# A GRU scan of 256 steps: the input product of r, z and n as one matmul of 192 columns, two pairs of steps ahead, over three sets of PSUM banks

## The chip, the cores and the metric

The kernel runs on one core of one Trainium2 chip. The metric is the time of one execution on the device in microseconds (us), median over several runs. TensorE (PE in the profile, PEld for its weight loads), VectorE (DVE), ScalarE (ACT), GpSimd (POOL) and SyncE (SP, which issues DMAs) each work through an instruction stream of their own, in order, and meet by semaphores.

## What is computed

`x` is 16 batches of 256 steps of 512 channels. First each channel is convolved over time with its own 16 taps (causally; the taps of a channel are its 16 batch values of `cond`) and the result is added to `x`. Then a GRU runs over the 256 steps, with `cond` as the first state, and its states are added to that `x`:

```python
gi = x @ W_ih + b_ih          # 512 -> 3 * 512, known ahead of the step
gh = h @ W_hh + b_hh          # needs the state of the step before
r = sigmoid(i_r + h_r)
z = sigmoid(i_z + h_z)
n = tanh(i_n + r * h_n)
h = (1 - z) * n + z * h
```

All of it is float32.

## The kernel before

**Layout.** The 512 channels are four chunks c of 128, and a chunk is four column groups j of 32 on the PE. State and `x` are stored with channels on partitions. The output channels are worked in two halves f (256 channels each), so that one half's gates can be computed while the PE is on the other.

**PE, one step t** (L321 to L340). `recur(t, f, c)` (L286) multiplies the state, as the 32 stationary columns (16 batches of two steps, one of which is zero), with 192 columns of `whh`: r, z and n of half f. It is issued for eight pairs (f, c) in a fixed order, of which the first needs `s_h[0]` (half 0 of the state before) and the fourth `s_h[1]`. Behind them come four of the eight calls of `product(m + 1, t % 2, c)` (L262): the input product of the next pair of steps, half 0 in the even step and half 1 in the odd one. A product is two sets of four matmuls: 128 columns for r and z into `pg[m % 2][f]`, at L278, and 64 columns for n into a bank of its own, `pin[m % 2]`, at L281. The sums of r and z are made in PSUM on top of the product. The part of n of the input has to stay apart from that of the state, as the state's is multiplied by r first. `turn` (L295) makes, for steps 16 to 79 of x, the convolution on the PE in four sets of 16 rounds, which are spread over the steps named in `ROUNDS`.

**ACT** first seeds the PSUM banks with the biases (`seed`, L344: two copies of 192 columns at L353 and one of 128 at L354 for each pair, at the end of the odd steps), since the matmuls only add. Per step and half it computes sigmoid for r and z (L379), 1 - z (L381) and tanh (L384).

**DVE** has in each step, in this order (L503 to L519): for half 0 the transposes of r and z (`transpose_rz`, L446) and of the state's n (`transpose_n`, L450) out of PSUM and the scan that gives r * h_n + i_n (`scan_n`, L458); the transposes of half 1; `scan_h` of half 0 (L471), which gives the new state and releases the PE by `s_h[0]`; `scan_n` and `scan_h` of half 1, which gives `s_h[1]`. Then, in odd steps, `transpose_in` (L441): the input's n of the next pair, 128 columns out of `pin`. Last come parts of the convolution for later steps: `spread` (L437), and `long` (L423), one instruction per step or so from step 13 to 206 (`SPANS`).

**POOL** multiplies z by the state (L253) and adds the state to x for the output (L247). **SP** loads weights and x and stores the output in its own order.

The only place at which the PE waits for DVE in a step is for the state:

```python
pe.wait_ge(s_h[0], t + 1)
recur(t, 0, 0)
recur(t, 0, 1)
recur(t, 1, 0)
pe.wait_ge(s_h[1], t + 1)
```

Of the kernel before, what the change touches and what calls it, by code (L numbers as in the profile page):

```python
# [32 lines left out]
M2 = T // 2  # L33
HN, END = 2 * CH * D, 3 * CH * D
STORES = [(n * TB, (n + 1) * TB) for n in range(NB - 1)] + [(T - 16, T - 8), (T - 8, T - 2), (T - 2, T)]


def build(nc, x, cond, w_ih, w_hh, b_ih, b_hh, out):
    assert J * D == P
    ctx = ExitStack()  # L40
    with ctx:  # L41
# [23 lines left out]
        bhh = sb("bhh", [P, 3 * C])  # L65
        bcol = sb("bcol", [P, H, 3, CH])
        bc = sb("bc", [P, H, END])
        bcn = sb("bcn", [P, C * D])
# [4 lines left out]
        gn = sb("gn", [P, 2, H, CH, B, 2])  # L73
        rz = sb("rz", [P, H, 2, HB, 2])
# [32 lines left out]
        s_x1 = sem("s_x1")  # L107
        s_seed = sem("s_seed")
        s_gi = sem("s_gi")
        s_tin = sem("s_tin")  # L110
        s_gh = halves("s_gh")
# [45 lines left out]
        def _(sp):  # L157
# [103 lines left out]
        def _(pe):  # L261
            def product(m, f, c):  # L262

                if f == c == 0:
                    pe.wait_ge(s_seed, 3 * (m + 1))
                    if 2 * m < FEW:
                        pe.wait_ge(s_first, len(FIRST))
                    elif 2 * m < TB:
                        pe.wait_ge(s_first, len(FIRST) + len(REST))
                        pe.wait_ge(s_pa, K)  # L270
                    elif 2 * m < LONG[0][0]:
                        pe.wait_ge(s_x1, 2 * NT * ((2 * m - TB) // W2 + 1))
                    else:
                        pe.wait_ge(s_long, len(EVERY) * sum(a <= 2 * m for a, _ in LONG))
                w = wih[:, c, :, :].rearrange("p (g k) (j d) -> p j g k d", g=3, j=J)[:, :, :, f * CH:(f + 1) * CH]
                xx = x1_of(c, 2 * m, 2 * m + 2)
                for j in range(J):
                    pe.matmul(pg[m % 2][f][D * j:D * (j + 1), 0:HN], xx, w[:, j, 0:2],  # L278
                              start=False, stop=True, skip_group_check=True)
                for j in range(J):  # L280
                    i = pe.matmul(pin[m % 2][D * j:D * (j + 1), f * CH * D:(f + 1) * CH * D], xx, w[:, j, 2],  # L281
                                  start=False, stop=True, skip_group_check=True)
                if f == H - 1 and c == C - 1:
                    i.then_inc(s_gi, 1)

            def recur(t, f, c):  # L286

                for j in range(J):
                    i = pe.matmul(pg[t // 2 % 2][f][D * j:D * (j + 1), 0:END],  # L289
                                  hp[:, t % 2, 2 * c + 1 - t % 2:2 * c + 3 - t % 2, :, 1].rearrange("p u b -> p (u b)"),  # L290
                                  whh[:, c, :].rearrange("p (g j f n) -> p j f g n", g=3, j=J, f=H)[:, j, f],
                                  start=False, stop=True, skip_group_check=True)
                return i
# [16 lines left out]
            pe.wait_ge(s_clear, 1)  # L310
            for q in range(2):
                for bank in (pg[q][0], pg[q][1], pin[q]):
                    pe.matmul(bank[:, :], zeros[:, 0:P], zeros[:, :], start=True, stop=True).then_inc(s_bits, 1)
            for _ in range(WARM):
                pe.matmul(pcv[:, 0:512], zeros[:, 0:P], zeros[:, :], start=True, stop=True)
            for f in range(H):
                for c in range(C):
                    if f == 0:
                        pe.wait_ge(s_wih[c], 16)
                    product(0, f, c)  # L320
            for t in range(T):  # L321
                m = t // 2
                for c in range(C if t == 0 else 0):
                    pe.wait_ge(s_whh[c], 16)
                pe.wait_ge(s_h[0], t + 1)
# [17 lines left out]
        def _(act):  # L343
            def seed(m):  # L344

                if m < 2:
                    act.wait_ge(s_bits, 6)
                    act.wait_ge(s_bc, H + 1)
# [3 lines left out]
                for f in range(H):  # L352
# [18 lines left out]
            act.activation(pre[:, :], cnd[:, 0, :], ACT.Sigmoid)  # L371
            seed(0)
            seed(1)
            act.wait_ge(s_zero, 4)
            for t in range(T):
                u = slice(t % 2 * B, (t % 2 + 1) * B)
                for f in range(H):
# [6 lines left out]
                    act.activation(nzh[:, f, ::2, :, 0], chunks(an[:, f, :, 1]), ACT.Tanh).then_inc(s_n[f], 1)  # L384
                if t % 2 and t + 3 < T:
                    seed((t + 3) // 2)

        @block.vector
        def _(dve):
# [48 lines left out]

            def transpose_in(m):
                dve.wait_ge(s_gi, m + 1)  # L440
                dve.transpose(gn[:, :, :, :, :, 1].rearrange("p u f c b -> p (f c) u b"),  # L441
                              pin[m % 2][:, 0:C * D]).then_inc(s_tin, 1)

            def transpose_rz(t, f):
                dve.wait_ge(s_gh[f], t + 1)
                dve.transpose(gt[:, f, :, :].rearrange("p c r -> p (c r)"),  # L446
                              pg[t // 2 % 2][f][:, 0:HN]).then_inc(s_trz[f], 1)

            def transpose_n(t, f):
                dve.transpose(gn[:, :, f, :, :, 0].rearrange("p u c b -> p c u b"),  # L450
                              pg[t // 2 % 2][f][:, HN:END]).then_inc(s_tn[f], 1)

            def scan_n(t, f):

                dve.wait_ge(s_rz[f], t + 1)
                dve.wait_ge(s_tn[f], t + 1)
                dve.wait_ge(s_tin, t // 2 + 1)
                dve.tensor_tensor_scan(an[:, f].rearrange("p n s -> p (n s)"),  # L458
                                       rz[:, f, 0].rearrange("p n s -> p (n s)"),
                                       gn[:, t % 2, f].rearrange("p c b s -> p (c b s)"),  # L460
                                       0.0, ALU.mult, ALU.add).then_inc(s_an[f], 1)
# [21 lines left out]
            dve.wait_ge(s_small, 32)  # L483
            dve.tensor_copy(bcol[:, :, 2, :], bhh[:, 2 * C:].rearrange("p (f k) -> p f k", f=H)).then_inc(s_bcol, 1)
            for g in range(2):
                dve.tensor_tensor(bcol[:, :, g, :], bih[:, g * C:(g + 1) * C].rearrange("p (f k) -> p f k", f=H),
                                  bhh[:, g * C:(g + 1) * C].rearrange("p (f k) -> p f k", f=H),
                                  ALU.add).then_inc(s_bcol, 1)
            dve.wait_ge(s_bcol, 3)
            for f in range(H):  # L490
                dve.transpose(bc[:, f, :].rearrange("p (k d) -> p k d", d=D),
                              bcol[:, f].rearrange("p s k -> p (s k)").unsqueeze(2).to_broadcast([P, 3 * CH, D])
                              ).then_inc(s_bc, 1)
            dve.transpose(bcn[:, :].rearrange("p (k d) -> p k d", d=D),
                          bih[:, 2 * C:].unsqueeze(2).to_broadcast([P, C, D])).then_inc(s_bc, 1)
            dve.wait_ge(s_xs, 16)
# [4 lines left out]
            dve.wait_ge(s_zero, 4)  # L501
            transpose_in(0)
            for t in range(T):  # L503
# [48 lines left out]
```

## Time and profile before

| | before |
|---|---|
| median of 3 runs | 1063.55 us (1062.34 to 1065.3) |
| profiled execution, own time | 1064.67 us |
| its span | 1062.9 us |
| PE busy | 1035.6 us, 97% |
| DVE busy | 781.8 us, 74% |
| ACT busy | 410.1 us, 39% |
| POOL busy | 246.5 us, 23% |
| mean granted clock of the PE | 0.996 |

The span is the part of the execution that the profile shows; 1.77 us of the execution's own time lie around it. A matmul of the program appears as two records in the profile, each with its weight load (16384 records for 8192 `recur` matmuls). Matmul ends are modelled, so the length of the PE's work is best read from one start to another.

### The profile page before, as it was taken

What the parts mean: (1) busy time and instruction counts of PE and PEld (TensorE: products, weight loads), DVE (VectorE), ACT (ScalarE), POOL (GpSimd) and SP (SyncE); (2) the same over time, 40 slices, a digit from 0 to 9 for tenths busy, and PEclk for the clock granted to TensorE, in tenths of its full rate; (3) what the DMA queues carried; (4) which work ended last, traced back from release to release, by engine and by line L of the source; (5) the groups of instructions that cost most, each with busy time, mean ns of one, the idle gap of its engine ahead of it and who ended that gap; (6) DMA issues with size and microseconds to landing.
All of it is one profiled execution on the core that took longest, in us unless ns stands there. A gap on an engine that the chain in (4) does not pass through costs nothing.

```text
span 1062.9 us, 74575 instructions
## 1 busy us (share of the span) xinstructions
PE 1035.6 (97%) x33336; PEld 964.1 (91%) x33336; DVE 781.8 (74%) x2474; ACT 410.1 (39%) x1939; POOL 246.5 (23%) x796
## 2 busy tenths in 40 slices
PE   8979998999999999999999999999999999999997
PEld 4867897999999988999999999999999999999997
DVE  8535786788888878888888877777777765555554
ACT  4323333334334334334444344343443434334443
POOL 6211221222222222222222222222222222222222
PEclk9999999999999999999999999999999999999999
DMA  7886003000000030000000000000000000000000
GB/s 273 80 154 63 24 5 113 13 5 24 5 25 5 11 95 5 24 5 25 5 4 25 5 25 5 24 5 5 25 4 24 5 17 12 4 24 5 25 15 13
DMA packets 96225, 32.60 MB, mean 31 GB/s; under 512 B 84512, under 2 KB 93344, under 8 KB 95904
## 3 DMA queue, kind: packets, MB, share of 16 engines
q1 hardware_dynamic: 95472, 27.73, 11.6%
q8 instruction: 261, 4.28, 1.7%
q14 instruction: 60, 0.49, 0.2%
q10 hardware_dynamic: 432, 0.11, 0.0%
HBM read 19.35 MB, written 8.49 MB: 26 GB/s over the span
## 4 chain that ended last, share of the span: by engine, by line
PE 96%; issue 2%; DMA 2%; SPq 0%; DVE 0%; POOLq 0%; ACT 0%; DVEq 0%
PE pg L289 64%; PE pg L278 21%; PE pin L281 10%; DMA whh<-w_hh 2%; PE pcv L304 1%; SPq L184 0%; SPq L186 0%; DVE hp L471 0%; SPq L182 0%; DVE gn L450 0%; SPq L181 0%; POOLq L41 0%; DVE an L458 0%; ACT nzh L384 0%; DVEq L469 0%
## 5 line engine op out<-in xcount | busy, mean ns | idle before, releaser
L289 PE MATMUL pg<-whh,hp 128*32 128x192 f32 x16384 | 752.9, 327 | 18.9 <-issue 14.9
L289 PEld LDWEIGHTS pg<-whh,hp 128*32 128x32 f32 x16384 | 609.6, 110 | 76.7 <-issue 25.2
L278 PE MATMUL pg<-wih,x 128*32 128x128 f32 x8192 | 391.6, 273 | 0.8 <-issue 0.7
L281 PE MATMUL pin<-wih,x 128*32 128x64 f32 x8192 | 363.4, 219 | 0.0
L253 POOL TENSOR_TENSOR nzh<-rz,hp 128x32 f32<-128x32 f32 x512 | 158.2, 309 | 806.5 <-ACT rz L379 806.5
L281 PEld LDWEIGHTS pin<-wih,x 128*32 128x32 f32 x8192 | 344.4, 110 | 0.0
L379 ACT ACTIVATE rz<-gt 128x64 f32<-128x64 f32 x512 | 136.4, 266 | 514.2 <-DVE gt L446 486.7
L278 PEld LDWEIGHTS pg<-wih,x 128*32 128x32 f32 x8192 | 326.6, 110 | 5.4 <-issue 1.5
L446 DVE STREAM_TRANSPOSE gt<-pg 128x128 f32<-128x128 f32 x512 | 162.0, 316 | 143.9 <-PE pg L289 135.1
L471 DVE TENSOR_TENSOR_SCAN hp<-zcp,nzh 128x96 f32<-128x96 f32 x512 | 173.2, 338 | 78.2 <-ACT nzh L384 78.0
L458 DVE TENSOR_TENSOR_SCAN an<-rz,gn 128x64 f32<-128x64 f32 x512 | 149.3, 292 | 52.7 <-ACT rz L379 51.8
L384 ACT ACTIVATE nzh<-an 128x32 f32<-128x32 f32 x512 | 121.5, 237 | 127.9 <-DVE an L458 127.9
L423 DVE SCALAR_TENSOR_TENSOR x<-xb,cnd,x 128x1024 f32<-128x1024 f32 (+1 forms) x120 | 134.1, 1118 | 0.0
L381 ACT ACTIVATE zcp<-gt 128x32 f32<-128x32 f32 x512 | 111.2, 217 | 0.0
L450 DVE STREAM_TRANSPOSE gn<-pg 128x64 f32<-128x64 f32 x512 | 107.2, 209 | 0.0
L247 POOL TENSOR_TENSOR x<-x,hp 128x64 f32<-128x64 f32 x256 | 81.8, 319 | 0.9 <-DVE hp L471 0.7
L423 DVE SCALAR_TENSOR_TENSOR x<-tz,cnd,x 128x1024 f32<-128x1024 f32 x60 | 75.2, 1253 | 0.0
L353 ACT ACTIVATE pg<-bc 128x192 f32<-128x192 f32 x256 | 72.9, 317 | 0.0
L441 DVE STREAM_TRANSPOSE gn<-pin 128x128 f32<-128x128 f32 x128 | 37.5, 293 | 0.0
L354 ACT ACTIVATE pin<-bcn 128x128 f32<-128x128 f32 x128 | 33.4, 261 | 0.0
L304 PE MATMUL pcv<-tz,xw 128*32 128x64 f32 x512 | 11.2, 220 | 1.7 <-issue 1.7
L407 DVE SCALAR_TENSOR_TENSOR x<-xs,cnd,x 128x192 f32<-128x192 f32 (+11 forms) x45 | 12.8, 361 | 0.0
(38 smaller groups left out, 87.6 us busy)
## 6 DMA issues: line engine op xcount, KB each, us to landing
out<-x SPq DMA_DIRECT2D x15, 512.0 KB, 4.8
xw<-x SPq DMA_DIRECT2D x32, 128.0 KB, 4.9
wih<-w_ih SPq DMA_DIRECT2D x4, 768.0 KB, 8.2
whh<-w_hh SPq DMA_DIRECT2D x4, 768.0 KB, 13.5
xb<-x SPq DMA_DIRECT2D x1, 2528.0 KB, 11.7
tz<-x SPq DMA_DIRECT2D x1, 2528.0 KB, 12.4
xb<-x SPq DMA_DIRECT2D x1, 2016.0 KB, 11.0
tz<-taps SPq DMA_DIRECT2D x8, 128.0 KB, 5.0
```

The source lines that it names most:

```text
L253: pool.tensor_tensor(nzh[:, f, ::2, :, 1], chunks(rz[:, f, 1, :, 1]), h_of(t - 1, slice(f * CH, (f + 1) * CH)), ALU.mult).then_inc(s_zh[f], 1)
L278: pe.matmul(pg[m % 2][f][D * j:D * (j + 1), 0:HN], xx, w[:, j, 0:2], start=False, stop=True, skip_group_check=True)
L281: i = pe.matmul(pin[m % 2][D * j:D * (j + 1), f * CH * D:(f + 1) * CH * D], xx, w[:, j, 2], start=False, stop=True, skip_group_check=True)
L289: i = pe.matmul(pg[t // 2 % 2][f][D * j:D * (j + 1), 0:END], hp[:, t % 2, 2 * c + 1 - t % 2:2 * c + 3 - t % 2, :, 1].rearrange("p u b -> p ...
L379: act.activation(rz[:, f, :, :, 1].rearrange("p g (c b) -> p (g c) b", b=B), gt[:, f, :, u], ACT.Sigmoid).then_inc(s_rz[f], 1)
L381: act.activation(zcp[:, f, ::2, :, 1], gt[:, f, CH:, u], ACT.Sigmoid, scale=-1.0).then_inc(s_zc[f], 1)
L384: act.activation(nzh[:, f, ::2, :, 0], chunks(an[:, f, :, 1]), ACT.Tanh).then_inc(s_n[f], 1)
L423: dve.scalar_tensor_tensor(o, xx[:, c, (K - 1 - lag) * B:(K - 1 - lag + n) * B], cnd[:, c, K - 1 - lag:K - lag], o if lag else now, ALU.mu ...
L446: dve.transpose(gt[:, f, :, :].rearrange("p c r -> p (c r)"), pg[t // 2 % 2][f][:, 0:HN]).then_inc(s_trz[f], 1)
L450: dve.transpose(gn[:, :, f, :, :, 0].rearrange("p u c b -> p c u b"), pg[t // 2 % 2][f][:, HN:END]).then_inc(s_tn[f], 1)
L458: dve.tensor_tensor_scan(an[:, f].rearrange("p n s -> p (n s)"), rz[:, f, 0].rearrange("p n s -> p (n s)"), gn[:, t % 2, f].rearrange("p c ...
L471: dve.tensor_tensor_scan(hp[:, (t + 1) % 2, a:a + n].rearrange("p c b s -> p (c b s)"), zcp[:, f, 0:n].rearrange("p c b s -> p (c b s)"), ...
```

## The change

The input product of a pair is one matmul of 192 columns per (f, c, j), for r, z and n together, into the one bank `pg[m % 3][f]`. A bank now holds, in 256 columns, the state's n (0 to 64), r and z (64 to 192) and the input's n (192 to 256). `recur` writes columns 0 to 192, `product` columns 64 to 256. `pin` is gone, and there are three sets of two banks instead of two sets of three (with `pcv` seven banks in both). Before the first step the products of pairs 0 and 1 are made, and step t makes half `t % 2` of pair `m + 2`.

`seed` is two copies of 256 columns for each pair, three pairs ahead. `transpose_in` is one instruction of 64 columns for each half: half 0 of the next pair at the end of the even step, half 1 at the end of the odd step, behind `scan_h(t, 1)`. `gn`, its target, has two buffers. Since `transpose_in` reads a bank that `recur` of the next pair writes, the PE waits in even steps for both transposes before the first `recur`. `whh` is loaded with n's columns first, in two DMAs per chunk. The rounds of `turn`, the `spread`s and the spans of `long` are one or two steps earlier.

```diff
-HN, END = 2 * CH * D, 3 * CH * D
+RZ, IN, END = CH * D, 3 * CH * D, 4 * CH * D
+Q = 3
...
-        pg = [[pb(f"pg{q}{f}") for f in range(H)] for q in range(2)]
-        pin = [pb(f"pin{q}") for q in range(2)]
+        pg = [[pb(f"pg{q}{f}") for f in range(H)] for q in range(Q)]
...
-        ROUNDS = {(0, 0): (7, 9), (0, 1): (11, 12), (1, 0): (16, 20), (1, 1): (28, 32)}
-        TURNED = {(0, 0): (9, 11), (0, 1): (12, 14), (1, 0): (20, 28), (1, 1): (32, 40)}
-        SPANS = [(13, 78), (78, 142), (142, 206)]
+        ROUNDS = {(0, 0): (7, 8), (0, 1): (10, 11), (1, 0): (16, 20), (1, 1): (28, 32)}
+        TURNED = {(0, 0): (8, 10), (0, 1): (11, 12), (1, 0): (20, 28), (1, 1): (32, 40)}
+        SPANS = [(12, 76), (76, 140), (140, 204)]
...
-                sp.dma_start(whh[:, c, :], w_hh[:, c, :]).then_inc(s_whh[c], 16)
+                sp.dma_start(whh[:, c, 0:F], w_hh[:, c, 2 * F:]).then_inc(s_whh[c], 16)
+                sp.dma_start(whh[:, c, F:], w_hh[:, c, 0:2 * F]).then_inc(s_whh[c], 16)
...
-                if f == c == 0:
-                    pe.wait_ge(s_seed, 3 * (m + 1))
+                if c == 0:
+                    pe.wait_ge(s_seed[f], m + 1)
...
                 for j in range(J):
-                    pe.matmul(pg[m % 2][f][D * j:D * (j + 1), 0:HN], xx, w[:, j, 0:2],
-                              start=False, stop=True, skip_group_check=True)
-                for j in range(J):
-                    i = pe.matmul(pin[m % 2][D * j:D * (j + 1), f * CH * D:(f + 1) * CH * D], xx, w[:, j, 2],
-                                  start=False, stop=True, skip_group_check=True)
-                if f == H - 1 and c == C - 1:
-                    i.then_inc(s_gi, 1)
+                    i = pe.matmul(pg[m % Q][f][D * j:D * (j + 1), RZ:END], x1_of(c, 2 * m, 2 * m + 2),
+                                  wih[:, c, :, :].rearrange("p (g k) (j d) -> p j g k d", g=3, j=J)
+                                  [:, j, :, f * CH:(f + 1) * CH],
+                                  start=False, stop=True, skip_group_check=True)
+                if c == C - 1:
+                    i.then_inc(s_gi[f], 1)
...
             for t in range(T):
                 m = t // 2
...
+                if t % 2 == 0:
+                    pe.wait_ge(s_tin[0], m + 1)
+                    pe.wait_ge(s_tin[1], m + 1)
                 pe.wait_ge(s_h[0], t + 1)
...
-                if m + 1 < M2:
+                if m + 2 < M2:
                     for c in range(C):
-                        product(m + 1, t % 2, c)
+                        product(m + 2, t % 2, c)
...
-                    act.wait_ge(s_tn[0], 2 * m - 2)
-                    act.wait_ge(s_tn[1], 2 * m - 2)
-                for f in range(H):
-                    act.activation(pg[m % 2][f][:, 0:END], bc[:, f, :], ACT.Copy).then_inc(s_seed, 1)
-                act.activation(pin[m % 2][:, 0:C * D], bcn[:, :], ACT.Copy).then_inc(s_seed, 1)
+                    act.wait_ge(s_tn[f], 2 * (m - Q) + 2)
+                act.activation(pg[m % Q][f][:, 0:END], bc[:, f, :], ACT.Copy).then_inc(s_seed[f], 1)
...
-            def transpose_in(m):
-                dve.wait_ge(s_gi, m + 1)
-                dve.transpose(gn[:, :, :, :, :, 1].rearrange("p u f c b -> p (f c) u b"),
-                              pin[m % 2][:, 0:C * D]).then_inc(s_tin, 1)
+            def transpose_in(m, f):
+                dve.wait_ge(s_gi[f], m + 1)
+                dve.transpose(gn[:, m % 2, :, f, :, :, 1].rearrange("p u c b -> p c u b"),
+                              pg[m % Q][f][:, IN:END]).then_inc(s_tin[f], 1)
...
-                if t % 2 and t + 1 < T:
-                    transpose_in((t + 1) // 2)
+                if t // 2 + 1 < M2:
+                    transpose_in(t // 2 + 1, t % 2)
```

## Rows read from the trace of the kernel before

**Rows 1.** The page: busy times, granted clock, chain that ended last.
```profile
PE 1035.6 (97%) x33336; PEld 964.1 (91%) x33336; DVE 781.8 (74%) x2474; ACT 410.1 (39%) x1939; POOL 246.5 (23%) x796
...
PEclk9999999999999999999999999999999999999999
...
PE 96%; issue 2%; DMA 2%; SPq 0%; DVE 0%; POOLq 0%; ACT 0%; DVEq 0%
```

**Rows 2.** Who waited for whom: us in total, times, longest.
```profile
PEld pg L289 <- issue: 25.2, 22, 4.2
...
PE pg L289 <- DMA whh<-w_hh: 3.1, 1, 3.1
```

**Rows 3.** The same view, PE alone, from 200 to 1050 us.
```profile
PE pg L289 <- issue: 1.9, 1, 1.9
```

**Rows 4.** Timeline, odd step and next start: start, us, engine, line, what [idle before].
```profile
1039.89 0.33 PE L289 MATMUL pg<-whh,hp 128*32 128x192 f32 x2
...
1041.87 0.32 DVE L446 STREAM_TRANSPOSE gt<-pg 128x128 f32<-128x128 f32 x1 [1.34 <-PE pg L289]
1042.10 0.21 DVE L450 STREAM_TRANSPOSE gn<-pg 128x64 f32<-128x64 f32 x1
...
1042.49 0.41 PE L278 MATMUL pg<-wih,x 128*32 128x128 f32 x6
...
1043.81 0.33 PE L289 MATMUL pg<-whh,hp 128*32 128x192 f32 x2
...
1044.09 0.36 DVE L471 TENSOR_TENSOR_SCAN hp<-zcp,nzh 128x96 f32<-128x96 f32 x1 [0.30 <-ACT nzh L384]
1044.36 0.29 DVE L441 STREAM_TRANSPOSE gn<-pin 128x128 f32<-128x128 f32 x1
1044.46 0.26 ACT L354 ACTIVATE pin<-bcn 128x128 f32<-128x128 f32 x1
1045.79 0.32 DVE L446 STREAM_TRANSPOSE gt<-pg 128x128 f32<-128x128 f32 x1 [1.13 <-PE pg L289]
```

**Rows 5.** Timeline, steps 254 and 255, which make no product.
```profile
1053.62 0.32 DVE L446 STREAM_TRANSPOSE gt<-pg 128x128 f32<-128x128 f32 x1 [1.13 <-PE pg L289]
...
1054.97 0.32 DVE L471 TENSOR_TENSOR_SCAN hp<-zcp,nzh 128x96 f32<-128x96 f32 x1
...
1055.34 2.81 PE L289 MATMUL pg<-whh,hp 128*32 128x192 f32 x64 [0.79 <-DVE hp L471]
...
1057.24 0.32 DVE L446 STREAM_TRANSPOSE gt<-pg 128x128 f32<-128x128 f32 x1 [1.05 <-PE pg L289]
```

**Rows 6.** Timeline of DVE in the stage with long convolutions.
```profile
500.91 0.32 DVE L446 STREAM_TRANSPOSE gt<-pg 128x128 f32<-128x128 f32 x1 [0.16 <-PE pg L289]
...
503.41 0.29 DVE L441 STREAM_TRANSPOSE gn<-pin 128x128 f32<-128x128 f32 x1
...
503.62 1.25 DVE L423 SCALAR_TENSOR_TENSOR x<-tz,cnd,x 128x1024 f32<-128x1024 f32 x1
504.83 0.32 DVE L446 STREAM_TRANSPOSE gt<-pg 128x128 f32<-128x128 f32 x1
```

**Rows 7.** Groups by line: busy, mean ns | idle; then the page's instruction queue of the PE.
```profile
L281 PE MATMUL pin<-wih,x 128*32 128x64 f32 x8192 | 363.4, 219 | 0.0
...
L353 ACT ACTIVATE pg<-bc 128x192 f32<-128x192 f32 x256 | 72.9, 317 | 0.0
L441 DVE STREAM_TRANSPOSE gn<-pin 128x128 f32<-128x128 f32 x128 | 37.5, 293 | 0.0
...
q8 instruction: 261, 4.28, 1.7%
```

**Rows 8.** Windows: us, busy (instructions) of PE, PEld, DVE, ACT, POOL; PEclk, DMA share, GB/s.
```profile
22.60:28.20 5.60, 5.60 (x129) 5.06 (x133) 4.06 (x21) 1.07 (x6) 0.62 (x2) 0.70 0.77 74
...
66.40:72.00 5.60, 2.86 (x105) 2.63 (x108) 1.75 (x8) 1.33 (x7) 0.91 (x3) 1.00 1.00 343
...
58.10:186.00 127.90, 114.02 (x3846) 101.78 (x3835) 83.86 (x269) 41.13 (x197) 23.43 (x78) 1.00 0.38 71
```

**Rows 9.** Timeline of the start.
```profile
16.65 0.43 PE L278 MATMUL pg<-wih,x 128*32 128x128 f32 x8 [0.70 <-issue]
...
22.60 4.49 PE L289 MATMUL pg<-whh,hp 128*32 128x192 f32 x64 [3.10 <-DMA whh<-w_hh]
...
24.67 0.31 DVE L441 STREAM_TRANSPOSE gn<-pin 128x128 f32<-128x128 f32 x1
```

More of the change, by code:

```diff
@@ L65, in build @@
         bhh = sb("bhh", [P, 3 * C])
-        bcol = sb("bcol", [P, H, 3, CH])
+        bcol = sb("bcol", [P, H, 4, CH])
         bc = sb("bc", [P, H, END])
-        bcn = sb("bcn", [P, C * D])
         pre = sb("pre", [P, B])
@@ L72, in build @@
         gt = sb("gt", [P, H, G, D])
-        gn = sb("gn", [P, 2, H, CH, B, 2])
+        gn = sb("gn", [P, 2, 2, H, CH, B, 2])
         rz = sb("rz", [P, H, 2, HB, 2])
@@ L107, in build @@
         s_x1 = sem("s_x1")
-        s_seed = sem("s_seed")
-        s_gi = sem("s_gi")
-        s_tin = sem("s_tin")
+        s_seed = halves("s_seed")
+        s_gi = halves("s_gi")
+        s_tin = halves("s_tin")
         s_gh = halves("s_gh")
@@ L310, in _ @@
             pe.wait_ge(s_clear, 1)
-            for q in range(2):
-                for bank in (pg[q][0], pg[q][1], pin[q]):
-                    pe.matmul(bank[:, :], zeros[:, 0:P], zeros[:, :], start=True, stop=True).then_inc(s_bits, 1)
+            for q in range(Q):
+                for f in range(H):
+                    pe.matmul(pg[q][f][:, :], zeros[:, 0:P], zeros[:, :], start=True, stop=True).then_inc(s_bits, 1)
             for _ in range(WARM):
                 pe.matmul(pcv[:, 0:512], zeros[:, 0:P], zeros[:, :], start=True, stop=True)
-            for f in range(H):
[L317 to L320, printed above, removed]
+            for m in range(2):
+                for f in range(H):
+                    for c in range(C):
+                        if m == f == 0:
+                            pe.wait_ge(s_wih[c], 16)
+                        product(m, f, c)
             for t in range(T):
@@ L323, in _ @@
                 for c in range(C if t == 0 else 0):
-                    pe.wait_ge(s_whh[c], 16)
+                    pe.wait_ge(s_whh[c], 32)
+                if t % 2 == 0:
+                    pe.wait_ge(s_tin[0], m + 1)
+                    pe.wait_ge(s_tin[1], m + 1)
                 pe.wait_ge(s_h[0], t + 1)
@@ L343, in _, with seed @@
         def _(act):
[L344 to L348, printed above, removed]
-                else:
-                    act.wait_ge(s_tn[0], 2 * m - 2)
-                    act.wait_ge(s_tn[1], 2 * m - 2)
-                for f in range(H):
-                    act.activation(pg[m % 2][f][:, 0:END], bc[:, f, :], ACT.Copy).then_inc(s_seed, 1)
-                act.activation(pin[m % 2][:, 0:C * D], bcn[:, :], ACT.Copy).then_inc(s_seed, 1)
+            def seed(m, f):
+                if m < Q:
+                    act.wait_ge(s_bits, 2 * Q)
+                    act.wait_ge(s_bc, H)
+                else:
+                    act.wait_ge(s_tn[f], 2 * (m - Q) + 2)
+                act.activation(pg[m % Q][f][:, 0:END], bc[:, f, :], ACT.Copy).then_inc(s_seed[f], 1)
             def tap_product(lag):
@@ L371, in _ @@
             act.activation(pre[:, :], cnd[:, 0, :], ACT.Sigmoid)
-            seed(0)
-            seed(1)
+            for m in range(Q):
+                for f in range(H):
+                    seed(m, f)
             act.wait_ge(s_zero, 4)
@@ L384, in _ @@
                     act.activation(nzh[:, f, ::2, :, 0], chunks(an[:, f, :, 1]), ACT.Tanh).then_inc(s_n[f], 1)
-                if t % 2 and t + 3 < T:
-                    seed((t + 3) // 2)
+                if t % 2 and t // 2 + Q < M2:
+                    for f in range(H):
+                        seed(t // 2 + Q, f)
         @block.vector
@@ L446, in transpose_rz @@
                 dve.transpose(gt[:, f, :, :].rearrange("p c r -> p (c r)"),
-                              pg[t // 2 % 2][f][:, 0:HN]).then_inc(s_trz[f], 1)
+                              pg[t // 2 % Q][f][:, RZ:IN]).then_inc(s_trz[f], 1)
             def transpose_n(t, f):
-                dve.transpose(gn[:, :, f, :, :, 0].rearrange("p u c b -> p c u b"),
-                              pg[t // 2 % 2][f][:, HN:END]).then_inc(s_tn[f], 1)
+                dve.transpose(gn[:, t // 2 % 2, :, f, :, :, 0].rearrange("p u c b -> p c u b"),
+                              pg[t // 2 % Q][f][:, 0:RZ]).then_inc(s_tn[f], 1)
             def scan_n(t, f):
@@ L456, in scan_n @@
                 dve.wait_ge(s_tn[f], t + 1)
-                dve.wait_ge(s_tin, t // 2 + 1)
+                dve.wait_ge(s_tin[f], t // 2 + 1)
                 dve.tensor_tensor_scan(an[:, f].rearrange("p n s -> p (n s)"),
                                        rz[:, f, 0].rearrange("p n s -> p (n s)"),
-                                       gn[:, t % 2, f].rearrange("p c b s -> p (c b s)"),
+                                       gn[:, t // 2 % 2, t % 2, f].rearrange("p c b s -> p (c b s)"),
                                        0.0, ALU.mult, ALU.add).then_inc(s_an[f], 1)
@@ L483, in _ @@
             dve.wait_ge(s_small, 32)
-            dve.tensor_copy(bcol[:, :, 2, :], bhh[:, 2 * C:].rearrange("p (f k) -> p f k", f=H)).then_inc(s_bcol, 1)
+            dve.tensor_copy(bcol[:, :, 3, :], bih[:, 2 * C:].rearrange("p (f k) -> p f k", f=H)).then_inc(s_bcol, 1)
+            dve.tensor_copy(bcol[:, :, 0, :], bhh[:, 2 * C:].rearrange("p (f k) -> p f k", f=H)).then_inc(s_bcol, 1)
             for g in range(2):
-                dve.tensor_tensor(bcol[:, :, g, :], bih[:, g * C:(g + 1) * C].rearrange("p (f k) -> p f k", f=H),
+                dve.tensor_tensor(bcol[:, :, 1 + g, :], bih[:, g * C:(g + 1) * C].rearrange("p (f k) -> p f k", f=H),
                                   bhh[:, g * C:(g + 1) * C].rearrange("p (f k) -> p f k", f=H),
                                   ALU.add).then_inc(s_bcol, 1)
-            dve.wait_ge(s_bcol, 3)
+            dve.wait_ge(s_bcol, 4)
             for f in range(H):
                 dve.transpose(bc[:, f, :].rearrange("p (k d) -> p k d", d=D),
-                              bcol[:, f].rearrange("p s k -> p (s k)").unsqueeze(2).to_broadcast([P, 3 * CH, D])
+                              bcol[:, f].rearrange("p s k -> p (s k)").unsqueeze(2).to_broadcast([P, 4 * CH, D])
                               ).then_inc(s_bc, 1)
-            dve.transpose(bcn[:, :].rearrange("p (k d) -> p k d", d=D),
-                          bih[:, 2 * C:].unsqueeze(2).to_broadcast([P, C, D])).then_inc(s_bc, 1)
             dve.wait_ge(s_xs, 16)
@@ L501, in _ @@
             dve.wait_ge(s_zero, 4)
-            transpose_in(0)
+            transpose_in(0, 0)
+            transpose_in(0, 1)
             for t in range(T):
```

4 lines of the change are left out of this document (1 added, 3 removed).

## The prediction

> **What bounds the kernel now.** I read the page first: the PE is busy for 97% of the span at full clock, and the chain that ended last is 96% PE [rows 1]. That alone does not say whether the PE is full or just fed in time, so I went to the list of waits. Between 200 and 1050 us the PE waits once, for 1.9 us, and for nothing that another engine does [rows 3]. It is full. The other losses are 25.2 us of "issue" on its weight loads, all but a few us of it before 200 us, and 3.1 us for `whh` at the start [rows 2]. The timeline gives one step's make-up, from start to start: `recur` 1039.89 to 1042.49 = 2.60 us for eight groups of 192 columns, so 0.325 each; the product 1042.49 to 1043.81 = 1.32 us for four groups of 128 and four of 64; together 3.92 us [rows 4].
>
> The second thing to read is how late the state comes, because that decides what the PE may wait for unpunished. In the odd step the transpose of r and z of half 0 starts at 1041.87, and `scan_h` of half 1 ends at 1044.09 + 0.36 = 1044.45: 2.58 us behind it, and 0.64 us **after** the PE has begun the next step at 1043.81 [rows 4]. That costs nothing now, since only the fourth group needs half 1, at 3 x 0.325 = 0.98 us into the step. Half 0 has its own slack: step 254 makes no product, and there the cycle from one such transpose to the next is 1057.24 - 1053.62 = 3.62 us [rows 5], against 3.92 with a product, so about 0.2 to 0.3 us.
>
> **The width.** Four groups of 192 take the place of four of 128 and four of 64. The columns are the same; by the 0.325 us of the `recur` group, of the same shape, the product is 1.30 us instead of 1.32. So 0.02 us per step that the PE bounds, which will be every second one (below): 127 x 0.02 = **-2.5 us**. The bounds are 0 (the order of the moving columns differs: runs of 32) and 5.
>
> **The wait.** In every even step from 2 to 254 the PE waits, ahead of its first group, for `transpose_in` of half 1. DVE issues that in the odd step before, behind `scan_h` of half 1. Queued behind the wait are all eight `recur` groups and then the product; DVE's next transpose of r and z waits for them, so the whole loop does. The price: DVE's instruction behind `scan_h` starts at 1044.36, 2.49 us behind the transpose of r and z, and one of 64 columns takes 0.21 us [rows 4], so it ends at +2.70. From DVE's end to the PE's start I take step 255, where the PE really waited: `scan_h` ends at 1054.97 + 0.32 = 1055.29 and the matmul starts at 1055.34, +0.05; from there to the next transpose of r and z it is 1057.24 - 1055.34 = 1.90 us [rows 5]. Odd to even is then 2.70 + 0.05 + 1.90 = 4.65 us instead of 3.92: 0.73 x 127 = **+92.7 us**. This is the term that decides. The PE's own idle time per pair would be 0.7 to 0.8 us, since a full stream also starts 0.07 us ahead of its predecessor's end. Nothing covers it: the product of the odd step has been issued by then, and `turn` is there in few steps.
>
> Two further waits stand in front of the first group. Bounds for them are 0 and the 0.05 us of a release [rows 5]; I take the middle, 0.025 x 127 = **+3 us**.
>
> The wait itself cannot be argued away. In this trace no matmul writes a bank that DVE reads at that moment, so no row shows what it would do. The Trainium skill, PSUM — Partial Sum Buffer, section Terms, calls TensorE writing and VectorE reading the same bank and quadrant at once a collision that gives wrong data; by that rule the wait has to stand even though the columns differ, and the sum is as it is. If columns alone counted, the wait could be dropped and the sum would be without the 92.7 and the 3.
>
> **DVE and ACT otherwise.** One transpose of 128 columns (0.29 us, end of the odd step) becomes two of 64 (0.21 each). In even steps that puts one ahead of `long`. There, DVE's `long` starts 2.49 us behind the transpose of r and z where nothing stands between, about 0.13 later now (transposes of 64 overlap their successor), and takes 1.25: it ends at 3.87 against the 3.90 at which the next transpose is due [rows 6]. Free by 0.03 us; the bound, with the full 0.21, is 0.05 late in 96 even steps, +5 us. In odd steps the PE's wait gives DVE room. `seed` is two copies of 256 columns for 0.32 + 0.32 + 0.26: by the step from 128 to 192 columns, 0.26 to 0.32 [rows 4, 7], some 0.37 each, 0.74 in place of 0.90 us, three pairs ahead, at the end of the odd step while ACT has nothing else; cost nothing, and with that cover gone 0.7 us per pair. Pair `m + 2`'s seed is issued in the step before its product begins and has 2.6 us of `recur` ahead of it.
>
> **The convolution on the PE.** Each of the four sets of 16 rounds is 16 x 0.325 / 3 = 1.7 us and stays. What falls into odd steps (7, 17, 19, 29, 31) lies in the PE's new idle time: 0.75 + 4 x 0.43 = **-2.5 us**. DVE makes eight `spread`s in step 11 instead of four in 12 and 13 each; some 0.3 us, once, in an odd step, also with room. The earlier steps of x that the products need stand ready in the same order; `long` from step 12 needs `xb`, which is issued behind the first sixteen loads of `xw`; a wait there would be a few us, once.
>
> **Instruction supply.** The queue that brings the PE's instructions moves 4.28 MB [rows 7], which is 64 bytes for each of its 66,672 records [rows 1]. The 25.2 us of "issue" fall where x is being loaded: from 58 to 186 us the PE was given 7681 instructions in 127.9 us, 60 per us [rows 8], where 3.92 us per step want about 66. The change takes away the 8192 matmuls of 64 columns with their loads [rows 7], a quarter of the stream, so it wants some 195 in 4.28 us, 46 per us. That is under what was delivered, but the stalls come in bursts. Bounds: none goes, all 25 go. I take **-15 us**.
>
> **Start and end.** Product 1 is made ahead of step 0: 2.6 us that fit into the 3.1 us wait for `whh` [rows 2, 9]. The second DMA per chunk is 4 more issues on SP's queue, ahead of the taps, which wait anyway; `whh` itself is taken to land as before. Step 0 took 5.60 us at clock 0.70 behind that idle time [rows 8]; with the PE busy nearly until then the clock should be at its upper level. DVE then bounds it: its first input transpose started at 24.67 [rows 9], r and z follow at about 25.2, and step 1 starts near 27.0, not 28.2: **-1.2 us**. At the end step 252 has no product either: **-0.3**.
>
> **Sum:** -2.5 + 92.7 + 3 - 2.5 - 15 - 1.2 - 0.3 = +74.2 us, on the profiled execution's own 1064.67: 1138.9 us. That execution is 1.1 above the median of the three runs, so **1138 us**, 7% slower.
>
> **The rivals.**
>
> *Main case, 0.82*: as summed, 1125 to 1156 (issue stalls all gone and no extra cost of the waits, or all kept and twice that cost).
>
> *DVE late, 0.10*: the extra transpose pushes `long` past the next transpose of r and z. For it speaks that the margin is 0.03 us; against, that instructions on DVE overlap by some 0.05. +5 to +10 us, 1143 to 1148.
>
> *The PE's clock falls, 0.03*: a pause in every second step brings the lower level. For it: step 0 after 3.1 us of idleness was granted 0.70 and took 5.60 instead of 3.92 us. Against: between 66.4 and 72 us the PE stood for 2.7 us and was granted 1.00 [rows 8]. Its price is 1.68 x 127 = +213, so 1351 us.
>
> *The other side, 0.03*: the release by `transpose_in` comes before the PE has finished the odd step's product, so that the wait is free and what remains is the PE's gain: 1064.67 - 5 - 15 - 1.2 - 1.1, about 1042 us. It decides at a release no later than 3.92 - 1.90 = 2.02 us behind the transpose of r and z; the rows have 2.75. For it speaks only that DVE's order could be other than I read. The Trainium skill, Perfetto Trace Analysis, section Matmuls, says that matmul groups should rotate through banks so that their evacuation overlaps the next matmuls, and that larger matmuls are more efficient; both would make this change faster. The trace bears out the second by 0.02 us per step and has nothing for the first to win, as the PE waits for no bank [rows 3].
>
> *The change does not do what it says, 0.02*: matmuls of 192 columns with runs of 32 stream more slowly than `recur`'s; at the old 1.32 us that is +2.5 us, inside the main case.
>
> **Range and chances.** 1120 to 1158 us takes in the main case and the late DVE. About 0.3% (3 us) is what a measurement of this kernel can tell from no change. Slower: 0.96; the same: 0.01; faster: 0.03.
>
> **What the profile after would show.** The list of waits has the PE waiting for `transpose_in` some 127 times, about 0.7 us each, 90 us in all; PE busy falls to about 90%. The distance between transposes of r and z alternates: 3.90 out of the even step, 4.65 out of the odd. The product is 1.30 us. Between 58 and 186 us "issue" on the PE is under 15 us. The clock stays at its upper level. I am wrong if the distances do not alternate, if DVE is never the PE's releaser, or if the even steps are over 3.95.

## The result and the profile after

The changed kernel takes 1147.23 us, median of 4 runs (1143.84 to 1147.77), beside 1062.94 us for the kernel before in the same session. The ratio is 1.0795, 95% interval 1.0758 to 1.0831: slower, by 84 us. The profiled execution has a span of 1145.7 us.

The page of the changed kernel, busy times and granted clock, as [rows 1], and its instruction queue, as [rows 7]:

```profile
PE 1051.9 (92%) x25144; PEld 976.9 (85%) x25144; DVE 791.9 (69%) x2602; ACT 398.3 (35%) x1811; POOL 246.6 (22%) x796
...
PEclk9999999999999999999999999999999999999999
...
q8 instruction: 198, 3.24, 1.2%
```

A quarter of the PE's instructions is gone and the clock is up in every slice (two short falls, shown below, are too small for them), but the PE is busy for 92% of a longer span. The list of waits of the changed kernel says where it stands, as [rows 2]:

```profile
PEld pg L286 <- issue: 127.3, 128, 4.0
...
PE pg L286 <- issue: 76.6, 123, 3.1
...
PE pg L286 <- DVE gn L441: 7.1, 4, 3.6
```

L286 is `recur`, and 123 is close to the 127 even steps from 2 on. The view calls the releaser "issue" in nearly all of them, that is, nothing that it can name; one of these is a real stall of 3.1 us. The timeline of an odd step and the even step behind it, as [rows 4], is what shows the releaser (L446: transpose of r and z; L471: `scan_h`; L441: `transpose_in`):

```profile
1002.71 0.32 DVE L446 STREAM_TRANSPOSE gt<-pg 128x128 f32<-128x128 f32 x1 [1.19 <-PE pg L286]
...
1004.93 0.36 DVE L471 TENSOR_TENSOR_SCAN hp<-zcp,nzh 128x96 f32<-128x96 f32 x1 [0.30 <-ACT nzh L383]
1005.20 0.23 DVE L441 STREAM_TRANSPOSE gn<-pg 128x64 f32<-128x64 f32 x1
...
1005.53 2.81 PE L286 MATMUL pg<-whh,hp 128*32 128x192 f32 x64 [0.60 <-issue]
1007.42 0.32 DVE L446 STREAM_TRANSPOSE gt<-pg 128x128 f32<-128x128 f32 x1 [1.99 <-PE pg L286]
```

`transpose_in` ends at 1005.43, the first matmul starts at 1005.53, and from one transpose of r and z to the next it is 4.71 us here. Between two even steps' starts, for instance 37.12 and 45.73 in the group below, it is 8.61 us, so even to odd is 8.61 - 4.71 = 3.90:

```profile
37.12 2.81 PE L286 MATMUL pg<-whh,hp 128*32 128x192 f32 x64 [0.61 <-issue]
45.73 2.81 PE L286 MATMUL pg<-whh,hp 128*32 128x192 f32 x64 [0.60 <-issue]
```

The start of the changed kernel, as [rows 9], with the window of step 0's matmuls (columns as in [rows 8]), holds a second loss:

```profile
25.00 0.36 DVE L441 STREAM_TRANSPOSE gn<-pg 128x64 f32<-128x64 f32 x2
25.61 5.34 PE L286 MATMUL pg<-whh,hp 128*32 128x192 f32 x64 [3.64 <-DVE gn L441]
...
34.30 0.32 DVE L446 STREAM_TRANSPOSE gt<-pg 128x128 f32<-128x128 f32 x1 [1.56 <-PE pg L286]
```
```profile
25.61:30.70 5.09, 5.09 (x64) 3.56 (x68) 0.74 (x3) 0.61 (x3) 0.31 (x1) 0.50 0.95 88
```

Step 0 begins at 25.61 us instead of 22.60 and its `recur` takes 5.09 us at a granted clock of 0.50, the lower of the two levels (1.2 GHz), behind 3.64 us of idleness.

### The profile page after: what moved, and what is told of

The parts are those of the page before. It is cut to its first block, busy times and chain, and to the rows that moved or that the text cites. A ratio compares the mean times of both kernels' runs of the same rounds, so it can differ in the third digit from the quotient of the medians.

```text
span 1145.7 us, 58329 instructions
## 1 busy us (share of the span) xinstructions
PE 1051.9 (92%) x25144; PEld 976.9 (85%) x25144; DVE 791.9 (69%) x2602; ACT 398.3 (35%) x1811; POOL 246.6 (22%) x796
## 4 chain that ended last, share of the span: by engine, by line
PE 90%; issue 7%; DVE 2%; DMA 0%; ACT 0%; SPq 0%; DVEq 0%; POOLq 0%; POOL 0%
PE pg L286 61%; PE pg L276 28%; DVE x L407 1%; PE pcv L301 1%; DVE x L397 0%; DMA xs<-x 0%; DVE hp L471 0%; DVE an L458 0%; DVE gn L450 0%; ACT nzh L383 0%; DVE gt L446 0%; DVE gn L441 0%; ACT rz L378 0%; SPq L180 0%; POOL nzh L253 0%
## 5 line engine op out<-in xcount | busy, mean ns | idle before, releaser
L286 PE MATMUL pg<-whh,hp 128*32 128x192 f32 x16384 | 724.1, 328 | 85.5 <-issue 76.6
L286 PEld LDWEIGHTS pg<-whh,hp 128*32 128x32 f32 x16384 | 636.3, 110 | 143.9 <-issue 127.3
L276 PE MATMUL pg<-wih,x 128*32 128x192 f32 x8192 | 388.5, 327 | 1.6 <-issue 1.6
L446 DVE STREAM_TRANSPOSE gt<-pg 128x128 f32<-128x128 f32 x512 | 162.0, 316 | 216.4 <-PE pg L286 206.9
L471 DVE TENSOR_TENSOR_SCAN hp<-zcp,nzh 128x96 f32<-128x96 f32 x512 | 172.8, 338 | 79.4 <-ACT nzh L383 79.2
L450 DVE STREAM_TRANSPOSE gn<-pg 128x64 f32<-128x64 f32 x512 | 106.9, 209 | 0.0
L352 ACT ACTIVATE pg<-bc 128x256 f32<-128x256 f32 x256 | 86.1, 368 | 0.0
L441 DVE STREAM_TRANSPOSE gn<-pg 128x64 f32<-128x64 f32 x256 | 57.5, 225 | 0.0
L312 PE MATMUL pcv<-zeros 128*128 128x512 bf16 x50 | 11.2, 385 | 0.0
L312 PEld LDWEIGHTS pcv<-zeros 128*128 128x128 bf16 x50 | 5.1, 101 | 6.4 <-issue 0.8
L301 PEld LDWEIGHTS pcv<-tz,xw 128*32 128x32 f32 x512 | 9.3, 110 | 1.1 <-issue 1.0
```

The costliest lines, as they stand in the source:

```text
L276: i = pe.matmul(pg[m % Q][f][D * j:D * (j + 1), RZ:END], x1_of(c, 2 * m, 2 * m + 2), wih[:, c, :, :].rearrange("p (g k) (j d) -> p j g k d ...
L286: i = pe.matmul(pg[t // 2 % Q][f][D * j:D * (j + 1), 0:IN], hp[:, t % 2, 2 * c + 1 - t % 2:2 * c + 3 - t % 2, :, 1].rearrange("p u b -> p ...
L352: act.activation(pg[m % Q][f][:, 0:END], bc[:, f, :], ACT.Copy).then_inc(s_seed[f], 1)
L450: dve.transpose(gn[:, t // 2 % 2, :, f, :, :, 0].rearrange("p u c b -> p c u b"), pg[t // 2 % Q][f][:, 0:RZ]).then_inc(s_tn[f], 1)
L471: dve.tensor_tensor_scan(hp[:, (t + 1) % 2, a:a + n].rearrange("p c b s -> p (c b s)"), zcp[:, f, 0:n].rearrange("p c b s -> p (c b s)"), ...
```

## The experiments

Theory W is the prediction's: the PE waits for a transpose that DVE makes too late. Its rival, theory I, takes the list of waits at its word: "issue", so the PE's own queue. Each edit is against the changed kernel unless it says otherwise. The runs come from three sessions, in which the kernel before took 1062.94, 1062.29 and 1062.01 us, so times of different sessions can be set beside each other to about 1 us.

**1. The transposes one step earlier** (`e1_early`). Three sets and two pairs of lead allow it: half 0 of pair m + 2 is complete at the end of step 2m, half 1 at the end of step 2m + 1.

```diff
+            transpose_in(1, 0)
             for t in range(T):
...
-                if t // 2 + 1 < M2:
-                    transpose_in(t // 2 + 1, t % 2)
+                if t % 2 == 0 and t // 2 + 1 < M2:
+                    transpose_in(t // 2 + 1, 1)
+                if t % 2 == 1 and t // 2 + 2 < M2:
+                    transpose_in(t // 2 + 2, 0)
```

> The changed kernel with half 1's input transpose made in the even step and half 0's in the odd step before it, so both are done a step or more before the PE asks for them; the waits on the PE stay. Theory W (the PE waits for the transpose that DVE makes behind scan_h of half 1, 0.7 to 0.8 us in each of 127 even steps): the distance between transposes of r and z is 3.90 us in every step, PE idle in even steps is gone, 1049 us (1043 to 1055), below the kernel before by its narrower instruction stream and 0.02 us per step. Theory I (the profile names issue as the releaser: the extra wait instructions in the PE's queue or its instruction supply cost the time, whatever DVE does): nothing moves, 1140 to 1150 us.

1044.04 us, ratio to the kernel before 0.9828 (0.9799 to 0.9857). Every step is now alike. The timeline of `e1_early`, DVE, odd and even steps in turn:

```profile
997.15 0.32 DVE L446 STREAM_TRANSPOSE gt<-pg 128x128 f32<-128x128 f32 x1 [1.19 <-PE pg L286]
...
1001.05 0.32 DVE L446 STREAM_TRANSPOSE gt<-pg 128x128 f32<-128x128 f32 x1 [1.19 <-PE pg L286]
...
1003.54 0.23 DVE L441 STREAM_TRANSPOSE gn<-pg 128x64 f32<-128x64 f32 x1
1004.95 0.32 DVE L446 STREAM_TRANSPOSE gt<-pg 128x128 f32<-128x128 f32 x1 [1.19 <-PE pg L286]
```

The distances are 3.90 and 3.90. The wait instructions on the PE are all still there, and so are the PE's instructions (25144 matmul records in both): theory I has fallen, and 103.2 us between the two kernels are 0.81 us for each of 127 pairs, which is 4.71 - 3.90.

**2. The wait alone, in the kernel before** (`e2_before_wait`).

```diff
+                if t % 2 == 0:
+                    pe.wait_ge(s_tin, m + 1)
                 pe.wait_ge(s_h[0], t + 1)
```

> The kernel before with one wait added: the PE waits in even steps for the input transpose of the same pair (128 columns, behind scan_h of half 1 in the odd step). Nothing else of the change. Theory W: odd to even becomes 2.49 + 0.29 + 0.07 + 1.90 = 4.75 us instead of 3.92, 0.83 x 127 = 105 us more, 1168 us (1160 to 1172), a few us less where stalls of the instruction supply fall into the pause. Theory I (issue): one short wait instruction per pair, under 0.05 us each, at most 1070 us.

1160.61 us, ratio 1.0925 (1.0893 to 1.0957), 98 us over the kernel before. Its list of waits has lines of another numbering (L443 is `transpose_in`, L289 `recur`):

```profile
PE pg L289 <- DVE gn L443: 81.0, 124, 5.7
PE pg L289 <- issue: 6.2, 4, 3.4
```

and its timeline of DVE gives the transposes of r and z (L448) behind the odd and the even step:

```profile
1005.21 0.32 DVE L448 STREAM_TRANSPOSE gt<-pg 128x128 f32<-128x128 f32 x1 [1.34 <-PE pg L289]
...
1009.95 0.32 DVE L448 STREAM_TRANSPOSE gt<-pg 128x128 f32<-128x128 f32 x1 [1.96 <-PE pg L289]
```

4.74 us odd to even (4.75 expected), from one line of code. 0.82 x 127 is 104 us, and the transpose of step 1 is 2.3 us later (32.35 against 30.09); the two spans are 94.8 us apart, so some 11 us less were lost elsewhere. That stalls of the supply fall into the pauses had been expected, but as a few us: 1160.6 us is 7 below the 1168 forecast.

With one added wait the view names DVE; with the changed kernel's two it says "issue". The trace's records of semaphore instructions, which the views leave out, show why. The first weight load of an even step carries one of the step's waits itself; the others stand in a semaphore instruction in front of it, one per even step in both runs. In `e2_before_wait` that instruction waits for the state, is met and takes 0.05 us (the median), and the weight load carries the late wait. In the changed kernel the instruction holds the late wait, for half 1, beside the one for the state: it takes 1.06 us (the median), in the pair of steps shown above from 1004.41 to 1005.47, 0.04 us past the end of the transpose. The weight load itself waits only for half 0's transpose, done long before, so the view finds nobody. In `e1_early` the same instruction takes 0.05 us. The Trainium skill, Perfetto Trace Analysis, section Identifying Dependency Chains, has it that an instruction which waits for several engines may get semaphore instructions of its own in front, with the further conditions; the trace agrees, though the waits here are all for DVE.

**3. The dose in between** (`e6_ahead_of_scan`): half 1's transpose moves up by one place only.

```diff
                 scan_n(t, 1)
+                if t % 2 == 1 and t // 2 + 1 < M2:
+                    transpose_in(t // 2 + 1, 1)
                 scan_h(t, 1)
-                if t // 2 + 1 < M2:
-                    transpose_in(t // 2 + 1, t % 2)
+                if t % 2 == 0 and t // 2 + 1 < M2:
+                    transpose_in(t // 2 + 1, 0)
```

> The changed kernel with half 1's transpose in the odd step moved up by one place, in front of scan_h of half 1, where DVE stands 0.30 us for tanh. Theory W says the loss is linear in the moment of release: it ends about 2.10 us behind the transpose of r and z instead of 2.72, the PE starts 0.10 behind it and r and z follow 1.89 later, 4.09 us odd to even, 0.19 x 127 = 24 us over e1_early: 1068 us (1055 to 1075). If a wait costs a fixed amount whenever it is met late, it stays within 10 us of the changed kernel.

1062.68 us, ratio 1.0000 (0.9974 to 1.0025). The timeline of an odd step and the next even one in `e6_ahead_of_scan`:

```profile
1000.86 0.32 DVE L446 STREAM_TRANSPOSE gt<-pg 128x128 f32<-128x128 f32 x1 [1.18 <-PE pg L286]
...
1002.69 0.23 DVE L441 STREAM_TRANSPOSE gn<-pg 128x64 f32<-128x64 f32 x1
...
1004.91 0.32 DVE L446 STREAM_TRANSPOSE gt<-pg 128x128 f32<-128x128 f32 x1 [1.48 <-PE pg L286]
```

The release comes 2.06 us behind the first transpose instead of 2.72, and the next one 4.05 instead of 4.71: the loop follows the release one for one. 0.15 x 127 = 19 us over `e1_early`, and 18.6 measured. One place in DVE's order, into 0.30 us in which it stood for tanh anyway, is worth 85 us, and even so the PE is still 0.15 us late.

The same rule points at a remedy that was not tried. Only the third group of a step writes half 1's bank, so the wait for half 1's transpose could stand in front of that group and not of the first. An estimate from the changed kernel's rows: undisturbed, the third group would start 3.90 - 1.89 + 2 x 0.325 = 2.66 us behind the transpose of r and z, and the release is at 2.72 + 0.10, so some 0.16 us per pair would be lost in place of 0.81.

**4. The third set and the second pair of lead, taken away** (`e3_one_ahead`).

```diff
-Q = 3
+Q = 2
...
-            for m in range(2):
+            for m in range(1):
...
-                if m + 2 < M2:
+                if m + 1 < M2:
                     for c in range(C):
-                        product(m + 2, t % 2, c)
+                        product(m + 1, t % 2, c)
```

> The changed kernel with two sets of banks and the product one pair ahead instead of three sets and two pairs; width, waits and the place of the transposes stay. Theory W: the transpose of half 1 could not be earlier than now in this order anyway, and the product of the odd step ends before scan_h of half 1 does, so the third set and the second pair of lead buy nothing as they stand: the same distances of 3.90 and 4.71, 1141 to 1149 us. Rival: the lead is what keeps the wait as short as it is (the transpose would wait for the product of its own step): odd to even grows by over 0.1 us, 1160 us or more.

1146.74 us, ratio 1.0793 (1.0748 to 1.0838), the same as the changed kernel. The lead was paid for in banks and bought nothing, since the transpose was left where it was; only an earlier transpose (experiments 1 and 8) spends it.

**5. The width, with the wait out of the way** (`e4_early_split`, against `e1_early`): the product again as 128 and 64 columns, both into the same bank.

```diff
                 for j in range(J):
-                    i = pe.matmul(pg[m % Q][f][D * j:D * (j + 1), RZ:END], ...
+                    pe.matmul(pg[m % Q][f][D * j:D * (j + 1), RZ:IN], ...
+                for j in range(J):
+                    i = pe.matmul(pg[m % Q][f][D * j:D * (j + 1), IN:END], ...
```

> As e1_early, but with the product split again into 128 and 64 columns (both into the one bank). Theory W with my prices: 3.92 us per step instead of 3.90, 5 us, and the instruction stream has its old length, so stalls of about 25 us come back instead of about 10: 10 to 20 us over e1_early. If the width is worth nothing, it is within 3 us of e1_early.

1070.32 us, ratio 1.0063 (1.0037 to 1.0089), 26 us over `e1_early`, more than I had. The transposes of r and z of half 0 in its timeline (L451) are 3.92 us apart, so 0.02 x 253 = 5 us are the columns:

```profile
1000.83 0.32 DVE L451 STREAM_TRANSPOSE gt<-pg 128x128 f32<-128x128 f32 x1 [1.19 <-PE pg L291]
...
1004.75 0.32 DVE L451 STREAM_TRANSPOSE gt<-pg 128x128 f32<-128x128 f32 x1 [1.19 <-PE pg L291]
```

The rest is the instruction supply. The page has 4.29 MB on the PE's instruction queue, as in the kernel before, and the list of waits of the weight loads:

```profile
PEld pg L291 <- issue: 20.0, 18, 4.4
PEld pg L276 <- issue: 8.1, 4, 3.3
...
PEld pcv L306 <- issue: 1.4, 1, 1.4
```

against those of `e1_early`:

```profile
PEld pg L286 <- issue: 8.0, 4, 4.0
PEld pcv L301 <- issue: 1.9, 1, 1.9
PEld pg L276 <- issue: 1.8, 2, 0.9
```

29.5 us against 11.7 on these lines. They are no full account: of the 8.0 us, 4.0 stand in front of step 0, where the PE waits for DVE (experiment 6). The timelines give one. From the transpose of r and z of step 1 to that of step 255 it is 1058.81 - 31.71 = 1027.10 us here and 1035.38 - 32.78 = 1002.60 in `e1_early`: 24.5 us more, of which 5 are the columns and 19.4 are stalls, with what the clock lost behind them. With a step 1 that comes 1.1 us earlier this is the 23.4 us between the two spans (1064.4 and 1041.0). The medians are 26 us apart since the executions differ: the profiled one of this version took 1066.33 us, and its eight lie between 1065.74 and 1071.77.

**6. The start** (`e5_early_start`, against `e1_early`). In step 0 the added wait is for pair 0's transposes, which stood behind all of DVE's first convolution.

```diff
             for q in range(len(REST)):
+                if q == 33:
+                    transpose_in(0, 0)
+                    transpose_in(0, 1)
                 rest(q)
             dve.wait_ge(s_zero, 4)
-            transpose_in(0, 0)
-            transpose_in(0, 1)
```

> As e1_early, but the two transposes of pair 0's product stand among DVE's convolution instructions (in front of the 34th of 48), done before whh has landed. If the late start of step 0 (25.6 us in the changed kernel against 22.6) and the low clock behind it are due to the wait for them: recur starts at about 22.6 us, the clock of step 0 is at its upper level, and the time is 4 to 6 us below e1_early. If whh lands late because of its eight DMAs, it starts near 25 all the same and the time is equal.

1039.56 us, ratio to the kernel before 0.9793 (0.9764 to 0.9822), 4.5 us below `e1_early`. The timeline of its start, and the window as above:

```profile
22.06 0.36 DVE L441 STREAM_TRANSPOSE gn<-pg 128x64 f32<-128x64 f32 x2
...
23.38 2.81 PE L286 MATMUL pg<-whh,hp 128*32 128x192 f32 x64 [1.65 <-DMA whh<-w_hh]
...
27.28 2.81 PE L286 MATMUL pg<-whh,hp 128*32 128x192 f32 x64
```
```profile
22.60:28.20 5.60, 4.82 (x120) 4.76 (x124) 4.81 (x25) 1.24 (x6) 0.62 (x3) 1.00 0.75 71
```

`recur` starts when `whh` has landed, at 23.38 and not at 22.6, the clock is at its upper level, and step 0 takes 3.90 us. The transpose of r and z of step 1 stands at 29.17 us, against 32.78 in `e1_early`: 3.6 of the 4.5 us, and the rest is no more than what executions differ by. This version is faster than both kernels, than the one before by 2.1%.

**7. The price of a wait that is met** (`e7_no_waits`, against `e5_early_start`).

```diff
-                if t % 2 == 0:
+                if t == 0:
                     pe.wait_ge(s_tin[0], m + 1)
                     pe.wait_ge(s_tin[1], m + 1)
```

> As e5_early_start, with the two waits for the input's transposes left only in step 0 (in later steps s_h implies them, since DVE works in order). What do two wait instructions cost in the PE's queue when they are already met? Theory W: nothing, since the PE runs ahead of its array: the same as e5_early_start within 3 us. If they cost 0.02 to 0.05 us per pair even then, it is 3 to 6 us below e5_early_start.

1039.49 us against 1039.56: nothing that these runs (1038.4 to 1040.8 and 1037.75 to 1041.88) can tell.

**8. Is DVE late with one transpose more ahead of the long convolution?** (`e8_both_even`)

```diff
-                if t // 2 + 1 < M2:
-                    transpose_in(t // 2 + 1, t % 2)
+                if t % 2 == 0 and t // 2 + 1 < M2:
+                    transpose_in(t // 2 + 1, 0)
+                    transpose_in(t // 2 + 1, 1)
```

> The changed kernel with both input transposes of a pair at the end of the even step, ahead of the long convolution. The PE's wait is free as in e1_early, but DVE's convolution now ends at about 2.49 + 0.26 + 1.25 = 4.00 us behind the transpose of r and z, 0.10 late for the next one at 3.90, in 96 steps. If the slack of 0.2 to 0.3 us in the state's chain takes that up: within 3 us of e1_early, 1041 to 1048. If not: 10 us more, 1054.

1043.56 us, ratio 0.9829 (0.9788 to 0.9870), like `e1_early`. The timeline of DVE in the stage of the long convolutions:

```profile
502.45 0.32 DVE L446 STREAM_TRANSPOSE gt<-pg 128x128 f32<-128x128 f32 x1
...
504.94 0.36 DVE L441 STREAM_TRANSPOSE gn<-pg 128x64 f32<-128x64 f32 x2
505.22 1.24 DVE L423 SCALAR_TENSOR_TENSOR x<-tz,cnd,x 128x1024 f32<-128x1024 f32 x1
506.38 0.31 DVE L446 STREAM_TRANSPOSE gt<-pg 128x128 f32<-128x128 f32 x1
```

The convolution ends 4.01 us behind the first transpose, the next one starts at 3.93 (it overlaps the end). What is late comes back in the next distance: from step 40 to 200 they are 3.93 and 3.87 us in turn, 3.90 on the mean. So the slack of the state's chain takes it up, as in the first of the two expectations.

## Why the prediction was right, point by point

The forecast was 1138 us, 1120 to 1158, slower; measured 1147.23. The terms, against the profiled executions:

- **The wait**, +92.7 and +3 for the two more in front. The step as put: odd to even 2.70 + 0.05 + 1.90 = 4.65. Measured 4.71: the transpose ends at +2.72, the PE starts 0.10 us behind it and not 0.05, and the next transpose follows 1.89 later. The PE's own pause is 0.60 us and not 0.7 to 0.8, because the record of a product ends 0.21 us past the point at which a following group would start (1.51 against 1.30), not 0.07; the sum did not use it. The loss against 3.92 is 0.79 x 127 = 100 us where I had 96. Experiments 1, 2 and 3 show this term from three sides. The 0.025 us per pair that I took for the two waits was half of what the late one cost, 0.05 (the semaphore instruction of experiment 2), and met ones cost nothing that experiment 7 could tell.
- **Start**, -1.2. This step failed. I let the PE start step 0 at 22.6 us and took from [rows 9] only that DVE's transpose at 24.67 would bound r and z. I left out that the added wait holds in step 0 too, so that nothing of `recur` runs until 25.61, and that the PE then sits idle for 3.64 us and starts at the lower clock. The transpose of r and z in step 1 is at 34.30 us against 30.09 in the kernel before: +4.2 instead of -1.2. Part of that belongs to this execution: in `e1_early`, with the same wait in step 0, `recur` starts at 25.31, takes 3.97 us at a granted clock of 0.65, and step 1's transpose stands at 32.78, +2.7. `whh` was not as early as before either, since in experiment 6 it released the PE at 23.38 and not at 22.60. Experiment 6 gets 4.5 us back by the medians. It was the same rule, "what is queued behind the waiting instruction", that I had applied to the other 127.
- **Width**, -2.5: the even step is 3.90 instead of 3.92, as put.
- **Instruction supply**, -15, leaving 10 of 25. By the timeline of the changed kernel its steps add up to 1132.9 us (34.30 to step 1; 4.71; 126 x 8.61 less 0.3; 3.62; 5.63 behind the last), with 4.4 for the `turn` rounds 1137.3, of the span of 1145.7: 8.4 us are left. Nine odd steps from 141 on take 1.8 of them: `scan_h` of half 1 starts 0.2 us later there, for a reason that was not looked into, and the wait passes it on (751.98 to 756.90, 4.92 us, for one). The stalls are what remains, 6.6 us with what the clock lost behind one of them. So 18 us or more of the 25 went where I had 15, and experiment 5 shows that the shorter stream is the cause. That the stalls come from the loads of x on the same DMA engines is argued from where they fall, before 200 us, and was not tried.
- **The convolution**, -2.5: as put. Where four rounds stand in an odd step, the pause behind them is 0.16 us and not 0.60 (at 115.57), and the 4.4 us above are what is left of 6.9.
- **DVE late**, given 0.10: it did not happen, and experiment 8 shows that there is room for twice the transposes.
- **The clock falls**, 0.03: not from pauses of 0.6 us. The granted clock of the span is 0.995. It did fall twice, in step 0 behind 3.64 us of idleness, and behind the real stall of 3.09 us. The timeline of the PE in the changed kernel and the window behind it:

```profile
68.51 2.57 PE L286 MATMUL pg<-whh,hp 128*32 128x192 f32 x34 [3.09 <-issue]
...
70.00:74.00 4.00, 4.00 (x76) 3.56 (x72) 2.52 (x11) 1.09 (x6) 0.90 (x3) 0.69 0.80 96
```

The kernel before has such a place too: 3.97 us of idleness up to 186.01, and a granted clock of 0.65 from 186 to 190.
- **The other side**, 0.03: the release is at 2.72 + 0.10 us where 2.02 was the point of decision. The rule of the Trainium skill beside it, Perfetto Trace Analysis, section Matmuls (rotate through banks, use larger matmuls), gives what it promises only once the order allows it: experiment 4 shows the rotation worth nothing by itself, experiment 1 shows rotation and width together worth 18 us against the kernel before, and experiment 5 that without the width nothing of that is left.

The miss is 8.7 us (1147.6 for the profiled execution, 1138.9 forecast for it): 5.4 for the start and 4.6 for the release (0.06 x 127, less the 3 allowed for it), less 1.6 for stalls, 8.4 in all. That is small because the wait, at 100 us, was put right to 5; the start had the wrong sign, and the range was wide enough to hold it.

What the profile was to show held but for three items. "issue" stands where I expected `transpose_in` to be named; the view names it in four pauses only, and that comes near to my sign of being wrong, DVE never the releaser, though DVE is the releaser. These pauses are 0.60 us and some 77 us in all, not 0.7 and 90. And the clock fell in two short stretches.

## What to carry to other kernels

When two uses share a bank to save instructions, ask who has to be finished with it before the PE may enter, and where in that engine's order this stands: here the gain was 18 us (experiment 1) and the wait cost 100, and moving the transpose by one step in an order written by hand kept the first without the second. A deeper buffer does nothing until something is issued earlier because of it. And a wait added to a loop also holds in its first round, where nothing is in steady state.

## What had not been expected

- A list of waits can hide the engine: of the 123 pieces under "issue" in the changed kernel, 122 with 73.5 us end 0.10 us behind the transpose of half 1 and are DVE's, as 81.0 us in 124 pieces under DVE are in experiment 2. The count and the constant 0.60 us gave it away, real stalls of the supply being few and of up to 4 us.
- From DVE's end to the PE's start it is 0.05 us where the weight load carries the late wait ([rows 5], and 0.055 in experiment 2), and 0.10 where a semaphore instruction in front of it does, in the changed kernel and in experiment 3. The difference is the 0.05 us that such an instruction takes when it is met.
- 8192 records of matmuls of 64 columns, with their weight loads a quarter of the PE's stream, cost 26 us in experiment 5, of which 5 are columns and per-matmul time. In this program, written out in full, fewer instructions are worth more than what they execute.
